# The norms ahead of two MLPs: from a stage of their own into the MLPs' first two chunks

## The chip, the cores and the metric

One core of one Trainium2 chip runs one program. The metric is the device time of that program in microseconds (us). A core has TensorE (PE in the profile, with its weight loads as PEld), VectorE (DVE), ScalarE (ACT), GpSimd (POOL), and SyncE (SP), which here only issues DMAs. Each engine works through its own list of instructions in order; they meet only in counters ("semaphores") that an instruction raises and another waits for.

## The reference, cut to what matters

Four layers are applied in turn to x, four batches of 512 tokens by 512 features. The second and the third layer each end in an MLP with a norm ahead of it, and these two places are changed:

```python
def ada_rms(x, t, w, tw):                       # layer 1
    n = x * jax.lax.rsqrt(jnp.mean(jnp.square(x), axis=-1, keepdims=True) + EPS)
    scale = t @ tw.T
    return n * (w * (1.0 + scale))[:, None, :]
h = ada_rms(x, time_emb, ln2_w, ln2_tw)
mlp = jax.nn.silu(h @ Wg.T) * (h @ Wu.T) @ Wd.T     # 512 -> 2048 -> 512
return res + mlp

def _ln(x):                                      # layer 2
    m = jnp.mean(x, axis=-1, keepdims=True)
    v = jnp.mean((x - m) ** 2, axis=-1, keepdims=True)
    return (x - m) / jnp.sqrt(v + LN_EPS)
h = _gelu_tanh((_ln(x) * (scale2 + 1.0) + shift2) @ Wfc1.T + bfc1)
x = x + (h @ Wfc2.T + bfc2) * gamma2
```

Everything is float32. Each batch needs only its own norm.

## The kernel before, in words

x lies in SBUF with the features on the partitions, as four tiles of 128 x 512 per batch (tile c is `k.xs(b, c)`). A sum over features is then a matmul with a matrix of 1/512 (`k.ones`), which also spreads the result over all partitions, into one bank of PSUM.

The program is a list of phases. A phase starts on an engine only when all engines have ended the phase before it, apart from a few instructions that a norm is let ahead by. The phases are: the conditioning vectors; `layers01` (all of layer 0 and the attention of layer 1, one woven sequence); `norm1b`, four norms, one per batch; `mlp1`; `layer2` (the attention of layer 2, woven); `norm2b`, four norms; `mlp2`; `layer3`. "Woven" means a Python list of (stage, batch, engine, operation) from which each engine takes its own operations in the list's order; waits are derived from what an operation reads.

A norm (class `Norm`) ahead of MLP 1 does, per batch: four squares on ACT into `k.t1` (L117), four matmuls with `k.ones` that sum them (L87, two fp32 passes each), the square root on ACT (L119), a reciprocal on DVE (L99), four scalings on DVE (L102), then for each tile a rounded copy "high" on ACT (L132) and the rest "low" on DVE (L109). High and low together carry float32 through the faster matmul type: the MLP multiplies high by high, high by low and low by high (`three`). The norm ahead of MLP 2 is a layer norm: it has four matmuls for the mean first (L81) and four subtractions (L96), a shift on ACT after the scaling (L124), and on ACT the addition of a bias to x itself (L136).

An MLP (class `Mlp`) cuts its 2048 hidden features into 8 chunks. A step is one chunk j for one batch q; the steps run j outermost: (0,0), (0,1), (0,2), (0,3), (1,0) and so on, 32 steps. A step's up matmuls fill tiles t = 0 and 1 of the hidden layer (L970; 48 matmuls of 128x512 with a gate, in MLP 1, 24 without, in MLP 2). ACT applies silu or gelu (L996, L998), DVE multiplies by the other half in MLP 1 (L1029), ACT makes high (L1004) and DVE low (L1035). The down matmuls (L983, 24 of them) run one step later, and DVE adds each of their four results to x (L1043). The chunk's weights arrive by a DMA of SP, and DVE splits them into high and low as well (L1016, L1021): chunk 0 before the first step, chunk j+1 during chunk j.

## Time and profile before

| | us |
|---|---|
| median of 3 runs | 2855.88 (2855.48 to 2857.81) |
| the profiled execution, its own time | 2853.02 |
| its span | 2851.0 |
| PE busy | 2561.1 (90%) |
| DVE busy | 1257.6 (44%) |
| ACT busy | 1133.4 (40%) |
| POOL busy | 263.4 (9%) |
| mean granted clock of TensorE | 0.943 of full |

The span runs from the first to the last instruction of the profile; 2.0 us of the execution lie around it. A time in the rows below counts from the span's start. "Busy" adds up the durations of an engine's instructions; TensorE's clock is given as a share of 2.4 GHz, and 0.50 is its lower level of 1.2 GHz.

### The profile page before, as it was taken

What the parts mean: (1) busy time and instruction counts of PE and PEld (TensorE: products, weight loads), DVE (VectorE), ACT (ScalarE), POOL (GpSimd) and SP (SyncE); (2) the same over time, 40 slices, a digit from 0 to 9 for tenths busy, and PEclk for the clock granted to TensorE, in tenths of its full rate; (3) what the DMA queues carried; (4) which work ended last, traced back from release to release, by engine and by line L of the source; (5) the groups of instructions that cost most, each with busy time, mean ns of one, the idle gap of its engine ahead of it and who ended that gap; (6) DMA issues with size and microseconds to landing.
All of it is one profiled execution on the core that took longest, in us unless ns stands there. A gap on an engine that the chain in (4) does not pass through costs nothing.

```text
span 2851.0 us, 32766 instructions
## 1 busy us (share of the span) xinstructions
PE 2561.1 (90%) x13072; PEld 1549.5 (54%) x13072; DVE 1257.6 (44%) x2490; ACT 1133.4 (40%) x2422; POOL 263.4 (9%) x233
## 2 busy tenths in 40 slices
...
DMA packets 35687, 61.24 MB, mean 21 GB/s; under 512 B 5184, under 2 KB 18032, under 8 KB 35024
## 3 DMA queue, kind: packets, MB, share of 16 engines
...
## 4 chain that ended last, share of the span: by engine, by line
PE 53%; DVE 5%; ACT 5%; issue 0%; POOL 0%; DVEq 0%; ACTq 0%; POOLq 0%
PE banks L970 18%; PE banks L983 12%; PE banks L441 10%; PE banks L682 3%; PE banks L675 2%; PE banks L695 2%; PE banks L527 1%; DVE sb_Pr L740 1%; DVE sb_PT L747 1%; PE banks L81 1%; PE banks L598 1%; ACT sb_Pr L765 1%; PE banks L591 1%; PE banks L87 1%; ACT sb_experts L609 1%; DVE sb_Pb L99 0%
## 5 line engine op out<-in xcount | busy, mean ns | idle before, releaser
L970 PE MATMUL banks<-sb_H,sb_Ws 128*128 128x512 f32 x2304 | 536.9, 391 | 31.1 <-DVE sb_Ws L1021 30.9
L970 PEld LDWEIGHTS banks<-sb_H,sb_Ws 128*128 128x128 f32 x2304 | 435.2, 189 | 123.8 <-issue 32.5
L765 ACT ACTIVATE sb_Pr<-sb_Pr,sb_nmax 128x512 f32<-128x512 f32 (+3 forms) x512 | 326.0, 638 | 117.4 <-DVE sb_nmax L740 115.2
L682 PEld LDWEIGHTS banks<-sb_ident,sb_Pr 128*128 128x128 f32 x2176 | 251.6, 147 | 210.4 <-issue 90.0
L682 PE MATMUL banks<-sb_ident,sb_Pr 128*128 128x128 f32 x2176 | 327.5, 292 | 28.2 <-ACT sb_PT L770 21.9
L675 PE MATMUL banks<-sb_R 32*128 32x512 f32 (+4 forms) x1280 | 305.9, 602 | 45.1 <-DVE sb_nmax L740 30.3
L747 DVE COPY sb_PT<-banks 128x512 f32<-128x512 f32 (+3 forms) x320 | 195.3, 610 | 333.4 <-PE banks L682 330.8
L740 DVE CUSTOM_DVE_ANT_0 sb_Pr<-banks,sb_bias 128x512 f32<-128x512 f32 (+3 forms) x512 | 290.9, 581 | 92.9 <-PE banks L675 91.9
L983 PE MATMUL banks<-sb_hidH,sb_Ws 128*128 128x512 f32 x1024 | 325.2, 389 | 0.0
L770 ACT ACTIVATE sb_PT<-banks 128x512 f32<-128x512 f32 (+3 forms) x320 | 169.2, 529 | 349.5 <-PE banks L682 348.8
L441 PE MATMUL banks<-sb_hN,sb_W 128*128 128x512 f32 x576 | 273.3, 622 | 12.3 <-ACT sb_hN L382 9.6
L675 PEld LDWEIGHTS banks<-sb_R 32*128 32x128 f32 (+1 forms) x1280 | 105.3, 192 | 200.4 <-issue 80.8
L983 PEld LDWEIGHTS banks<-sb_hidH,sb_Ws 128*128 128x128 f32 x1024 | 192.1, 188 | 39.8
L983 PE MATMUL banks<-sb_hidL,sb_Ws 128*128 128x512 f32 x512 | 199.2, 389 | 0.0
L441 PEld LDWEIGHTS banks<-sb_hN,sb_W 128*128 128x128 f32 x576 | 110.7, 201 | 138.1 <-issue 125.1
L1035 DVE TENSOR_TENSOR sb_hidL<-sb_hN,sb_hidH 128x512 fp32r<-128x512 f32 x128 | 88.6, 692 | 205.8 <-ACT sb_hidH L1004 205.8
L441 PE MATMUL banks<-sb_A,sb_W 128*128 128x512 f32 x384 | 174.6, 600 | 3.4 <-DVE sb_hN L482 3.4
L695 PE MATMUL banks<-sb_PT,sb_V 128*32 128x256 f32 (+2 forms) x2304 | 169.7, 381 | 1.8 <-DVE sb_rsum L751 0.9
L1004 ACT ACTIVATE sb_hidH<-sb_hN 128x512 fp32r<-128x512 f32 x128 | 80.9, 632 | 186.3 <-DVE sb_hN L1029 184.2
L1029 DVE TENSOR_TENSOR sb_hN<-sb_t,banks 128x512 f32<-128x512 f32 x64 | 44.0, 687 | 247.9 <-PE banks L970 195.5
L998 ACT ACTIVATE sb_hN<-banks,sb_cols 128x512 f32<-128x512 f32 x64 | 44.0, 688 | 248.4 <-PE banks L970 248.4
L996 ACT ACTIVATE sb_t<-banks 128x512 f32<-128x512 f32 x64 | 38.3, 599 | 245.7 <-PE banks L970 245.7
...
## 6 DMA issues: line engine op xcount, KB each, us to landing
sb_WM<-in_L_cond_Wfc SPq DMA_DIRECT2D x16, 512.0 KB, 4.2
...
sb_WM<-in_L_cond_Wg SPq DMA_DIRECT2D x8, 512.0 KB, 3.4
sb_WM<-in_L_cond_Wu SPq DMA_DIRECT2D x8, 512.0 KB, 4.4
sb_WM<-in_L_cond_Wd SPq DMA_DIRECT2D x8, 512.0 KB, 3.6
...
```

The source lines that it names most:

```text
L441: mm = e.matmul(bank[:, columns], lhsT, rhs, start=start, stop=stop)
L675: mm = e.matmul(k.bank(n % 4)[:, 0:s.width(u)], s.q(b, c)[rows, i * P:(i + 1) * P], s.k(b, c)[rows, 0:s.width(u)], start=True, stop=True)
L682: mm = e.transpose(bank[:, j * P:(j + 1) * P], k.Pr[:, n % 6, j * P:(j + 1) * P], k.ident[:])
L695: mm = e.matmul(bank[rows, 2 * P * ip + skip:2 * P * (ip + 1)], s.v(b, j, s.vhead(c, hl)), s.PT[:, n % 2, hl, j, skip:2 * P], start=j == 0 ...
L740: ins = e.tensor_tensor_reduce(k.Pr[:, n % 6, 0:s.width(u)], S, k.bias[:, s.units[u][2], 0:s.width(u)], -1.0, 3.0e38, ALU.add, ALU.min, s. ...
L747: ins = e.tensor_copy(*s.turned(k, b, u))
L765: ins = e.activation(prob, prob if s.biased else k.bank(n % 4)[:, 0:s.width(u)], ACT.Exp, bias=s.stat(k, k.nmax, b, u), scale=-1.0 if s.bi ...
L770: ins = e.activation(*s.turned(k, b, u), ACT.Copy)
L970: mm = e.matmul(k.bank(s.ups * t + w), lhsT, rhs, start=i == 0, stop=i == len(mats) - 1)
L983: mm = e.matmul(k.bank(4 + m), lhsT, rhs, start=i == 0, stop=i == len(mats) - 1)
L1004: ins = e.activation(k.hidH[:, st % 2, t, :], k.hN[:, 2 * (st % 2) + t, :], ACT.Copy)
L1035: ins = e.tensor_tensor(k.hidL[:, st % 2, t, :], k.hN[:, 2 * (st % 2) + t, :], k.hidH[:, st % 2, t, :].bitcast(F32), ALU.subtract)
```

## The change

The class `Norm` (and the unused `Linear` and `joined`) goes. `PairNorm` takes its place as a stage of a woven sequence, and each MLP becomes such a sequence that holds its norms.

- The order of the steps: chunks 0 and 1 go batch by batch, (0,0), (1,0), (0,1), (1,1), (0,2), (1,2), (0,3), (1,3), and from chunk 2 on j is outermost as before.
- The norm of batch 0 stands ahead of the first step, with the split of chunk 0 between its parts. The norm of batch q+1 is cut into parts ("beats") that follow, one each, the parts of steps (0,q) and (1,q); what is left when step (1,q) ends follows there.
- The split of chunk 1 stands at the end of step (0,0), and that of chunk 2 at the end of step (1,3).
- The sums over the four tiles are made on POOL (three additions of tiles), and one matmul with `k.ones` replaces four. In the first MLP POOL adds the squares; in the second it adds x and the squares.
- 1/sqrt(v) is exp(-0.5 ln v), both on ACT, in place of a square root on ACT and a reciprocal on DVE.
- The tiles of the norm: `nt`, two new ones, for sums, logarithm and inverse root; for the scaled values one new tile `nh` in MLP 1 (each c waits for the low of c-1), and `t1` in MLP 2. The norm's matmuls use bank 7 in MLP 1, which the down matmuls of m = 3 use too, and bank 2 in MLP 2.
- A matmul group "up" of step (j,q) waits for the high and the low of all four tiles of batch q.
- All else in the diff is a change of form (`after` returns what to wait for, and the caller waits).

```diff
-class Norm(Step):
...
+class PairNorm:
+    def beats(s, b):
+        tail = [[("pe", "var", 0), ("act", "log", 0), ("act", "inverse", 0)]]
+        for c in range(C):
+            last = [("dve", "scale", c)] + ([] if s.rms else [("act", "shift", c)])
+            last += [("act", "high", c), ("dve", "low", c)]
+            tail.append(last + ([("act", "extra", c)] if s.extra else []))
+        squares = [[("act", "square", c)] + ([("pool", "vsum", c)] if c else []) for c in range(C)]
+        if s.rms:
+            return squares + tail
+        return [[("pool", "xsum", i) for i in range(3)], [],
+                [("pe", "mean", 0)] + [("dve", "centre", c) for c in range(C)]] + squares + tail
...
+    def pe(s, k, e, b, kind, i, after):
+        bank = s.tab.claim(e, s, b, kind, i, after)
+        for due in after(s.name, b, *(("xsum", 2) if kind == "mean" else ("vsum", C - 1))):
+            e.wait_ge(*due)
+        e.matmul(bank, k.ones[:], k.nt[:, 0, :], start=True, stop=True).then_inc(k.done["pe"], 1)
...
+    def act(s, k, e, b, kind, c, after):
...
+            if c > 1:
+                for due in after(s.name, b, "vsum", c - 1):
+                    e.wait_ge(*due)
+            ins = e.activation(n1 if c else n0, s.x(b, c) if s.rms else s.h(c), ACT.Square)
...
+            ins = e.activation(n1, s.tab.at[(s.name, b, "var", 0)], ACT.Ln, bias=s.eps, scale=1.0)
...
+            ins = e.activation(n0, n1, ACT.Exp, scale=-0.5)
...
-        s.S = NCH * B
...
+        s.steps = [(j, q) for q in range(B) for j in range(2)] + [(j, q) for j in range(2, NCH) for q in range(B)]
+        s.at_step = {jq: st for st, jq in enumerate(s.steps)}
...
+    def sequence(s):
+        splits = {}
+        for j in range(2, NCH):
+            free, first = s.at_step[(j - 2, B - 1)] + 1, s.at_step[(j, 0)]
+            for p in range(len(s.pieces)):
+                splits.setdefault(min(free + 1 + p % 2, first - 1), []).extend(s.split(j)[2 * p:2 * p + 2])
+        splits[0] = s.split(1)
+        lead, first = s.norm.beats(0), s.split(0)
+        seq = []
+        for i in range(max(len(lead), len(first))):
+            seq += [(s.norm, 0, *op) for op in (lead[i] if i < len(lead) else [])]
+            seq += [(s, 0, *op) for op in first[i:i + 1]]
+        waiting = []
+        for st in range(len(s.steps) + 1):
+            parts = []
+            if st < len(s.steps):
+                j, q = s.steps[st]
+                for t in range(2):
+                    parts.append([("pe", "up", (st, t, w)) for w in range(s.ups)] + [("act", "act", (st, t))] +
+                                 ([("dve", "gate", (st, t))] if s.gated else []) +
+                                 [("act", "hidden high", (st, t)), ("dve", "hidden low", (st, t))])
+                if j == 0 and q + 1 < B:
+                    waiting = [[(s.norm, q + 1, *op) for op in ops] for ops in s.norm.beats(q + 1)]
+            if st >= 1:
+                parts += [[("pe", "down", (st - 1, m)), ("dve", "add", (st - 1, m))] for m in range(C)]
+            parts.append(splits.get(st, []))
+            for ops in parts:
+                seq += [(s, 0, *op) for op in ops]
+                if waiting:
+                    seq += waiting.pop(0)
+            if st < len(s.steps) and s.steps[st][0] == 1:
+                for ops in waiting:
+                    seq += ops
+                waiting = []
+        return seq
...
-        norm1b = [Norm(k.xs, combc(1), None, eps6[:, 0:1], rms=True, pair=(k.HH, k.HL))]
+        norm1b = PairNorm("norm1b", k.xs, lambda c: k.nh[:, 0, :], combc(1), None, eps6[:, 0:1], k.HH, k.HL, rms=True)
...
-        norm2b = [Norm(k.xs, modc(28), modc(36), eps6[:, 0:1], pair=(k.HH, k.HL), extra=combc(2))]
+        norm2b = PairNorm("norm2b", k.xs, lambda c: k.t1[:, c, :], modc(28), modc(36), eps6[:, 0:1], k.HH, k.HL,
+                          extra=combc(2))
...
+        mlp1, woven_mlp1 = mlp("mlp1", True, split1, [(0, 2 * C * HC), (2 * C * HC, 2 * D)], 1, norm1b, 7)
+        mlp2, woven_mlp2 = mlp("mlp2", False, split2, [(0, 2 * C * HC)], 2, norm2b, 2,
+                               hbias=col["L2_cond_bfc1"], gamma=modc(20))
```

Three places show how the instructions now stand. The first is DVE in the second step of MLP 1. Before, that step, (0,1), held gate (L1029), low (L1035), the split of chunk 1's first piece (L1016, L1021) and the four additions to x (L1043):

```order
L1029 TENSOR_TENSOR sb_hN<-sb_t,banks 128x512
L1035 TENSOR_TENSOR sb_hidL<-sb_hN,sb_hidH 128x512
L1029 TENSOR_TENSOR sb_hN<-sb_t,banks 128x512
L1035 TENSOR_TENSOR sb_hidL<-sb_hN,sb_hidH 128x512
L1016 CAST sb_Ws<-sb_WM 128x2048
L1021 TENSOR_TENSOR sb_Ws<-sb_WM,sb_Ws 128x2048
L1043 SCALAR_TENSOR_TENSOR sb_x<-banks,sb_x 128x512 x4
```

Now the second step, (1,0), holds the end of batch 1's norm; a piece of its start stands here, from the split of chunk 1 (L1056, L1060) on. L1070 is the gate, L1079 the hidden low, L1092 an addition to x, L922 the scaling of one tile of the norm and L927 its low:

```order
L1056 CAST sb_Ws<-sb_WM 128x1024
L1060 TENSOR_TENSOR sb_Ws<-sb_WM,sb_Ws 128x1024
L1070 TENSOR_TENSOR sb_hN<-sb_t,banks 128x512
L1079 TENSOR_TENSOR sb_hidL<-sb_hN,sb_hidH 128x512
L1070 TENSOR_TENSOR sb_hN<-sb_t,banks 128x512
L1079 TENSOR_TENSOR sb_hidL<-sb_hN,sb_hidH 128x512
L1092 SCALAR_TENSOR_TENSOR sb_x<-banks,sb_x 128x512
L922 SCALAR_TENSOR_TENSOR sb_nh<-sb_x,sb_comb,sb_nt 128x512
L927 TENSOR_TENSOR sb_H<-sb_nh,sb_H 128x512
L1092 SCALAR_TENSOR_TENSOR sb_x<-banks,sb_x 128x512
L922 SCALAR_TENSOR_TENSOR sb_nh<-sb_x,sb_comb,sb_nt 128x512
```

Each addition is now followed by a scaling and a low of the norm, four times in a row, before DVE comes to the next step's gate.

The second place is DVE in MLP 2, with batch 2's norm in step (1,1). Before, in the same place of the list, there are only hidden lows (L1035), additions (L1043) and a split:

```order
L1035 TENSOR_TENSOR sb_hidL<-sb_hN,sb_hidH 128x512 x2
L1043 SCALAR_TENSOR_TENSOR sb_x<-banks,sb_mod,sb_x 128x512 x4
L1035 TENSOR_TENSOR sb_hidL<-sb_hN,sb_hidH 128x512 x2
L1016 CAST sb_Ws<-sb_WM 128x2048
L1021 TENSOR_TENSOR sb_Ws<-sb_WM,sb_Ws 128x2048
L1043 SCALAR_TENSOR_TENSOR sb_x<-banks,sb_mod,sb_x 128x512 x4
```

Now the four subtractions of the mean (L912) stand among step (0,1)'s additions, and the scalings and lows among those of step (1,1):

```order
L1092 SCALAR_TENSOR_TENSOR sb_x<-banks,sb_mod,sb_x 128x512
L912 TENSOR_TENSOR sb_t<-sb_x,banks 128x512 x4
L1092 SCALAR_TENSOR_TENSOR sb_x<-banks,sb_mod,sb_x 128x512 x3
L1079 TENSOR_TENSOR sb_hidL<-sb_hN,sb_hidH 128x512 x2
L922 SCALAR_TENSOR_TENSOR sb_t<-sb_t,sb_mod,sb_nt 128x512
L927 TENSOR_TENSOR sb_H<-sb_t,sb_H 128x512
L1092 SCALAR_TENSOR_TENSOR sb_x<-banks,sb_mod,sb_x 128x512
L922 SCALAR_TENSOR_TENSOR sb_t<-sb_t,sb_mod,sb_nt 128x512
L927 TENSOR_TENSOR sb_H<-sb_t,sb_H 128x512
```

The pattern of the last three rows goes on until all four tiles are done.

The third place is ACT in the same steps. Before, the norms stood together ahead of the MLP, where ACT went from one table of functions to the next once (L119 is the root, L124 the shift, L132 high, L136 the addition to x, L998 gelu, L1004 hidden high):

```order
L119 ACTIVATE sb_Pb<-banks,sb_eps 128x512
L124 ACTIVATE sb_hN<-sb_hN,sb_mod 128x512 x4
L132 ACTIVATE sb_H<-sb_hN 128x512 x4
L136 ACTIVATE sb_x<-sb_x,sb_comb 128x512 x4
L998 ACT_TABLE_LOAD
L998 ACTIVATE sb_hN<-banks,sb_cols 128x512
L1004 ACTIVATE sb_hidH<-sb_hN 128x512
```

Now the logarithm (L886) and the exponential (L890) stand between two gelus (L1034), with a table load ahead of each of the three; L882 is a square, L894 the shift, L898 high, L902 the addition to x, L1042 hidden high:

```order
L1034 ACTIVATE sb_hN<-banks,sb_cols 128x512
L1042 ACTIVATE sb_hidH<-sb_hN 128x512
L886 ACT_TABLE_LOAD
L886 ACTIVATE sb_nt<-banks,sb_eps 128x512
L890 ACT_TABLE_LOAD
L890 ACTIVATE sb_nt<-sb_nt 128x512
L1034 ACT_TABLE_LOAD
L1034 ACTIVATE sb_hN<-banks,sb_cols 128x512
L1042 ACTIVATE sb_hidH<-sb_hN 128x512
L894 ACTIVATE sb_t<-sb_t,sb_mod 128x512
L898 ACTIVATE sb_H<-sb_t 128x512
L902 ACTIVATE sb_x<-sb_x,sb_comb 128x512
```

The second gelu of the step now comes behind the exponential and a table load.

## Rows read from the trace of the kernel before

**Rows 1.** Busy time by stretch: before and in each MLP; stretch and length, engines (instructions), PEclk.

```profile
1002.60:1065.50 62.90, 21.53 (x33) 8.38 (x33) 40.03 (x41) 22.86 (x37) 0.00 (x0) 0.70 0.09 29
1065.50:1589.80 524.30, 524.21 (x2304) 433.59 (x2304) 205.87 (x284) 80.10 (x129) 0.00 (x0) 1.00 0.07 21
2268.70:2350.80 82.10, 36.58 (x65) 13.99 (x63) 48.53 (x55) 42.34 (x69) 0.00 (x0) 0.76 0.18 51
2350.80:2702.10 351.30, 351.06 (x1536) 289.90 (x1536) 158.45 (x205) 85.76 (x129) 0.00 (x0) 0.99 0.05 19
```

**Rows 2.** Timeline, norms ahead of MLP 1: start, length, engine, line, what [idle <-releaser].

```profile
1002.65 0.69 DVE L1314 SCALAR_TENSOR_TENSOR sb_x<-banks,sb_x 128x512 f32<-128x512 f32 x1 [2.74 <-PE banks L441]
...
1003.90 0.51 SPq L1606 DMA_DIRECT2D sb_WM<-in_L_cond_Wu  x1
...
1059.96 1.23 DVE L1016 CAST sb_Ws<-sb_WM 128x2048 fp32r<-128x2048 f32 x1
...
1064.15 1.23 DVE L1021 TENSOR_TENSOR sb_Ws<-sb_WM,sb_Ws 128x1024 fp32r<-128x1024 f32 x1
...
1065.52 23.73 PE L970 MATMUL banks<-sb_H,sb_Ws 128*128 128x512 f32 x96 [15.04 <-DVE sb_Ws L1021]
```

**Rows 3.** Groups of instructions: DVE in 1003:1066, then ACT in 2268:2351 (mean ns).

```profile
L102 DVE SCALAR_TENSOR_TENSOR sb_hN<-sb_x,sb_comb,sb_Pb 128x512 f32<-128x512 f32 x16 | 11.0, 748 | 0.1
...
L124 ACT ACTIVATE sb_hN<-sb_hN,sb_mod 128x512 f32<-128x512 f32 x16 | 10.8, 722 | 16.8 <-DVE sb_hN L102 16.8
```

**Rows 4.** Timeline, first norm of the kernel: POOL sums, TensorE, logarithm and exponential.

```profile
93.11 1.26 POOL L358 TENSOR_TENSOR sb_t<-sb_t 128x512 f32<-128x512 f32 x1
...
102.62 2.08 PE L342 MATMUL banks<-sb_t,sb_ones 128*128 128x512 f32 x2 [6.05 <-POOL sb_t L358]
104.73 0.69 ACT L376 ACTIVATE sb_Pb<-banks,sb_eps 128x512 f32<-128x512 f32 x1 [3.58 <-PE banks L342]
105.43 1.28 ACT L379 ACT_TABLE_LOAD   x1
106.73 0.63 ACT L379 ACTIVATE sb_Pb<-sb_Pb 128x512 f32<-128x512 f32 x1
```

**Rows 5.** DMA issues, us to landing: in 1000:1030, then in 2265:2300.

```profile
sb_WM<-in_L_cond_Wu SPq DMA_DIRECT2D x1, 512.0 KB, 5.2
...
sb_WM<-in_L_cond_Wfc SPq DMA_DIRECT2D x4, 512.0 KB, 5.3
```

**Rows 6.** Timeline of two steps in MLP 1, then of one in MLP 2.

```profile
1078.48 0.69 DVE L1029 TENSOR_TENSOR sb_hN<-sb_t,banks 128x512 f32<-128x512 f32 x1 [3.36 <-PE banks L970]
1079.20 0.63 ACT L1004 ACTIVATE sb_hidH<-sb_hN 128x512 fp32r<-128x512 f32 x1 [2.91 <-DVE sb_hN L1029]
1079.87 0.69 DVE L1035 TENSOR_TENSOR sb_hidL<-sb_hN,sb_hidH 128x512 fp32r<-128x512 f32 x1 [0.70 <-ACT sb_hidH L1004]
...
1094.82 0.68 DVE L1043 SCALAR_TENSOR_TENSOR sb_x<-banks,sb_x 128x512 f32<-128x512 f32 x1
...
2359.11 5.69 PE L970 MATMUL banks<-sb_H,sb_Ws 128*128 128x512 f32 x24 [0.17 <-ACT sb_hidH L1004]
...
2362.12 0.69 ACT L998 ACTIVATE sb_hN<-banks,sb_cols 128x512 f32<-128x512 f32 x1 [1.79 <-PE banks L970]
```

**Rows 7.** Timeline, around the norms ahead of MLP 2.

```profile
2268.76 0.75 DVE L1314 SCALAR_TENSOR_TENSOR sb_x<-banks,sb_mod,sb_x 128x512 f32<-128x512 f32 x1 [2.68 <-PE banks L441]
...
2270.06 0.50 SPq L1618 DMA_DIRECT2D sb_WM<-in_L_cond_Wfc  x1
...
2285.23 6.62 PE L81 MATMUL banks<-sb_x,sb_ones 128*128 128x512 f32 x8 [7.69 <-ACT sb_hN L124]
```

**Rows 8.** Granted clock by stretch, where the MLPs begin.

```profile
1066.00:1072.00 6.00, 6.00 (x21) 4.74 (x20) 0.00 (x0) 1.68 (x2) 0.00 (x0) 0.74 0.56 196
...
2350.00:2356.00 6.00, 5.16 (x12) 4.12 (x13) 0.70 (x1) 0.00 (x0) 0.00 (x0) 0.50 0.50 175
```

**Rows 9.** Timeline of TensorE in layer 3.

```profile
2741.78 5.33 PE L441 MATMUL banks<-sb_Y,sb_Wout 128*128 128x512 f32 x8 [3.14 <-ACT sb_Y L382]
```

732 lines of the change are left out of this document (358 added, 374 removed).

## The prediction, as it was put on record

> **What bounds the kernel now.** I read three views. The busy time by stretch comes first [rows 1]: in both MLPs TensorE is busy all the time (524.21 of 524.30 us, 351.06 of 351.30), and ahead of each lies a stretch in which it mostly waits for a norm, 62.9 and 82.1 us. That is the 145.0 us the change works on; all else in the 2853.0 us stays as it is. The timeline comes second [rows 2, 7]: the last addition to x of the layer before ends at 1003.3 (2269.5), MLP 1's first matmul starts at 1065.52, MLP 2's at 2350.8. The third, single rows of one pass of each kind, gives durations [rows 3, 4, 6]. MLP 1's 2304 matmuls in 524.3 us are 0.227 us each: 24 of them (one tile's ups with a gate, or a step's downs) take 5.44.
>
> So TensorE sets the end inside an MLP, and the question is what it waits for when norms stand there too. I take ends and starts from the rows: TensorE to another engine 0.29 (2359.11 + 12 x 0.227 to 2362.12 [rows 6]), another engine to TensorE 0.14 (1065.38 to 1065.52 [rows 2]), ACT to DVE or back 0.03 [rows 6], into or out of POOL 0.10. Passes of 128x512: scale 0.75, shift 0.72 [rows 3], high 0.63, low 0.69 [rows 6], POOL addition 1.26 [rows 4], a square as the exponential, 0.63. The 0.10 for POOL is an allowance of mine.
>
> **The lead, batch 0's norm.** MLP 1: two squares, three POOL additions, two more squares between them: 1003.4 + 1.25 + 3 x 1.37 + 2 x 0.66 = 1010.1. The one matmul took 2.08 on a TensorE that had paused [rows 4], to 1012.3; logarithm 0.69, table load 1.28, exponential 0.63 follow each other without a gap there (104.73, 105.43, 106.73), to 1015.0. The weights' split takes 5.42 (1059.96 to 1065.38) and starts when the DMA issued at 1003.90 has landed, 5.2 later [rows 5]: 1014.6, just hidden. Then four tiles in a chain, since one `nh` serves all and DVE queues low c ahead of scale c+1: 0.75+0.63+0.69+3x0.03 = 2.16 each, 8.6. Ups start at 1023.7 instead of 1065.5: **-41.8**.
>
> MLP 2: DVE's list has the split (3.56) ahead of the subtractions; its DMA, issued at 2270.06, lands after 5.3, so they start at 2278.9. The first square starts 0.8 later; two squares take 1.25, three POOL additions with two squares between them 5.4, the matmul 2.2, logarithm to exponential 2.65: 2291.2. The additions for the mean, 3 x 1.26 from 2269.6, and its matmul end earlier than the split. A tile's chain has the shift too: 2.91 each, 11.6. Ups at 2302.95 instead of 2350.8: **-47.9**.
>
> **What comes back, step by step.** Let U be the time when a step's ups end on TensorE. Its last hidden low ends at U + 2.35 (0.29 + 0.69 + 0.63 + 0.69 and two 0.03).
>
> - Step (0,0) to (1,0). Chunk 1's split is queued on DVE behind that low, and step (0,0) has no downs to cover it. MLP 1: 2.35 + 5.42 + 0.14 = **+7.9**. MLP 2: 2.35 + 3.56 + 0.14 = **+6.05**.
> - MLP 1, batch 1's norm, in step (1,0). The matmul stands right behind the ups, ACT does high (to U+1.6), loads a table, and has the exponential done at U+5.55. Then DVE alternates additions and tiles: 4 x 2.16 + 3 x 0.71 = 10.8, with 0.14 to U+16.45. The downs need 5.44: **+11.0**.
> - MLP 1, batches 2 and 3: their parts start a step earlier. TensorE, in order, comes to the norm's matmul at U+4.1, and POOL's last sum is ready at U+7.75 (high ends at 1.65, then three squares of 0.66 and three additions of 1.37). The matmul is 0.9, and the next down shares bank 7, so it waits for the logarithm, 0.95. The tiles themselves are hidden behind a whole step. 5.5 each: **+11.0**.
> - Chunk 2's split stands at the end of step (1,3), behind the last addition: 0.96 + 5.42 + 0.14 = **+6.55**; MLP 2 0.29 + 0.75 + 3.56 + 0.14: **+4.7**.
> - MLP 2, batch 1's norm: a layer norm has 12 parts, and step (0,0) takes only three, so all squares stand in step (1,0). The sum is ready at U+7.75 as above, the matmul takes 1.0, logarithm to exponential 2.65, and then come four tiles (11.6), nearly all behind the step's last addition: next ups at U+23.15, own work 5.44: **+17.7**.
> - MLP 2, batches 2 and 3. The squares follow the subtractions behind step (0,q)'s first addition, the sum is ready at U+10.6, exponential at U+14.7; the second gelu of step (1,q) is queued behind it with a table load, its low ends at U+18.1. Only then does the first tile start: 4 x 2.91 + 3 x 0.78 + 0.14 to U+32.2. TensorE has 3 x 5.44 to do in between: **+15.85** each, 31.7.
>
> Sum: MLP 1 -41.8 + 7.9 + 11.0 + 11.0 + 6.55 = -5.3. MLP 2 -47.9 + 6.05 + 17.7 + 31.7 + 4.7 = +12.3. Together **+7**. The POOL additions, the reciprocals that go (eight) and the 36 matmuls that go are counted in the leads or hidden; POOL has nothing else to do there (0.00 busy [rows 1]), and the DMAs of later chunks are issued as early as before or earlier.
>
> **The clock.** TensorE's granted clock is at its lower level, 1.2 GHz, after the waits ahead of an MLP (0.50 of full [rows 8]). The first 24 ups of MLP 2 took 8.10 where the next 24 took 5.69 [rows 6, 7], and MLP 1's first 96 took 23.73 for 21.8 [rows 2]: 2 to 2.7 lost per return. After 7.69 us of idling eight matmuls ran 6.62 us for about 3.5 at the full clock [rows 7], after 3.14 us in a loose stretch eight took 5.33 [rows 9]. Five of the new pauses are 7.9 us or longer (MLP 1's first two, one per batch in MLP 2): 2.3 each, 11.5. Three last about 4.7 to 6.5: no row says which way they go, from 0 to 2.7 each, and I take half, 3.5. Clock: **+15**, bounds 0 and 27 (ten pauses of 2.7, with those of 3.7 us ahead of a sum).
> The page "TensorE: Matmul & The Clock Gate" of the Trainium skill, section "HAM oscillation", tells of a loop whose every round starts at the lower clock because each round has a pause. By that rule every pause here would be paid, the upper bound; the trace agrees for the long ones.
>
> **The table loads.** In the trace a load costs its 1.28 and nothing more: the logarithm ends at 105.42, the exponential starts at 106.73 [rows 4]. About eight of the new loads stand on the path (the exponential's in both leads, in both batches 1 and in MLP 2's batches 2 and 3, and there gelu's too).
> The Trainium skill, "ScalarE: Activation LUTs", section "What ACT_TABLE_LOAD costs", adds a drain of about 1.38 us to each switch, 2.66 in all. By it the sum would be 11 higher. The trace disagrees.
>
> **Forecast.** 2853.0 + 7 + 15 = 2875 for the profiled execution; the median of the runs lies 2.9 above it, so **2878**. Slower.
>
> **Rivals.**
> 1. *The norms are hidden* (the faster side). If the tiles' chain of batches 1 to 3 ended before the downs did, all that is left of the price is the splits and the nine matmuls: 2856 - 90 + 25 + 9 = 2800. For it: ACT is busy 80 of 524 us in MLP 1 and DVE 206 [rows 1], so there is room on average. Against: the list gives DVE the tiles only among or behind the last downs. It decides in MLP 2, at batches 2 and 3: were the first tile there 15.9 us earlier, the sum without the clock would turn from +7 to -25. 4%.
> 2. *The clock holds through the new pauses.* 2856 + 7 = 2863. For it: only average rows speak of how TensorE behaves between 3 and 7 us. Against: 7.69 us cost it. 12%.
> 3. *Every pause costs the clock*, and waits on POOL are longer than I took: 7 + 27 = 2890. 14%.
> 4. *The chains overlap more than I count*, DVE's next scaling under ACT's work, 2 us less per norm and half the clock: 2856 - 7 + 7 = 2856, no change. 8%. *Some piece outruns its chain by more*, faster by over 0.2%: 3%, beside rival 1.
>
> Forecast itself 59%. Two runs of this kernel differ by under 0.1%; 0.2% is 5.7 us, what a measurement can tell from none. Faster 0.07 (rival 1 and the last), same 0.10 (rival 4 and the edge of 2), slower 0.83. The range goes from below rival 2 to rival 3: 2857 to 2891.
>
> **What would show it.** TensorE's first up at about 20 us after the layer before in MLP 1 and 33 in MLP 2; between the first steps pauses of 8 and 11 us in MLP 1, 6, then 13, 12, 12 in MLP 2, ended by DVE's low of a norm (L927) or a split (L1060); MLP 1 from the last addition before it to its end about as long as before, MLP 2 some 20 us longer; a clock at half in the first stretch behind each pause. It is wrong if TensorE's waits for L927 sum to under 30 us, or if the ups start later than 1030 and 2310.

## The result, and the profile after

The changed kernel takes 2884.15 us (median of 4 runs, 2882.56 to 2887.32) against 2855.68 us (4 runs, 2853.25 to 2857.81): ratio 1.0102, 95% interval 1.0087 to 1.0117. It is slower by 28.5 us; 22 were forecast. The profiled execution took 2882.56 us (span 2880.6).

Busy time by stretch of the changed kernel, one core; columns are stretch and length, then busy time (and instructions) of PE, PEld, DVE, ACT, POOL, then PEclk, DMA share, GB/s. The four stretches are MLP 1's lead and the rest of MLP 1, then the same of MLP 2. They answer to [rows 1].

```profile
1005.49:1026.74 21.25, 2.05 (x3) 0.53 (x3) 12.06 (x12) 9.68 (x13) 4.66 (x3) 0.61 0.45 148
1026.74:1600.30 573.56, 540.01 (x2310) 441.53 (x2310) 227.08 (x307) 109.07 (x168) 11.65 (x9) 0.96 0.05 17
2275.43:2309.72 34.29, 3.69 (x4) 0.83 (x5) 12.39 (x15) 15.37 (x21) 10.63 (x9) 0.57 0.52 153
2309.72:2732.90 423.18, 370.71 (x1548) 300.36 (x1548) 184.17 (x241) 131.05 (x192) 20.69 (x16) 0.93 0.04 13
```

The reader is to see three things. The leads are short now: 21.25 us where 62.2 lay between the same two events (1003.3 to 1065.5), 34.3 where there were 81.3. Behind them TensorE, which never waited inside an MLP before, is idle for 573.56 - 540.01 = 33.6 us in MLP 1 and 423.18 - 370.71 = 52.5 in MLP 2. And it is busy longer for the same work: 540.0 us, less 3 for the norms' three matmuls (two passes each, six of the 2310), against 524.2, and 370.7, less 6.2 for six matmuls, against 351.1. That is 12.8 and 13.4 us, 26.2 together, and its granted clock says why: 0.96 and 0.93 instead of 1.00 and 0.99.

From the last addition of the layer before to its last matmul, MLP 1 takes 594.8 us (586.4 before), MLP 2 457.5 (432.6). So the two stages lose 33.3; the layers that the change does not touch came out 3.7 shorter in this execution (layer 2 took 675.1 us instead of 679.8).

Where TensorE waits, in the timeline of the changed kernel; columns are start, length, engine, line, operation, out<-in, count, [idle before <-releaser]. L844 is a norm's matmul, L1016 an MLP's, L927 DVE's low of a norm, L1060 the split, L866 a POOL addition.

```profile
1026.74 13.01 PE L1016 MATMUL banks<-sb_H,sb_Ws 128*128 128x512 f32 x48 [11.52 <-DVE sb_H L927]
1049.42 13.54 PE L1016 MATMUL banks<-sb_H,sb_Ws 128*128 128x512 f32 x48 [9.67 <-DVE sb_Ws L1060]
...
1078.64 12.64 PE L1016 MATMUL banks<-sb_H,sb_Ws 128*128 128x512 f32 x48 [9.35 <-DVE sb_H L927]
1098.69 1.88 PE L844 MATMUL banks<-sb_nt,sb_ones 128*128 128x512 f32 x2 [3.34 <-POOL sb_nt L866]
...
2323.22 7.83 PE L1016 MATMUL banks<-sb_H,sb_Ws 128*128 128x512 f32 x24 [4.86 <-DVE sb_Ws L1060]
2338.61 2.05 PE L844 MATMUL banks<-sb_nt,sb_ones 128*128 128x512 f32 x2 [3.48 <-POOL sb_nt L866]
2356.35 8.30 PE L1016 MATMUL banks<-sb_H,sb_Ws 128*128 128x512 f32 x24 [13.14 <-DVE sb_H L927]
...
2396.77 8.53 PE L1016 MATMUL banks<-sb_H,sb_Ws 128*128 128x512 f32 x24 [12.53 <-DVE sb_H L927]
...
2436.45 7.54 PE L1016 MATMUL banks<-sb_H,sb_Ws 128*128 128x512 f32 x24 [11.55 <-DVE sb_H L927]
2449.27 5.60 PE L1016 MATMUL banks<-sb_H,sb_Ws 128*128 128x512 f32 x24
2464.71 7.07 PE L1016 MATMUL banks<-sb_H,sb_Ws 128*128 128x512 f32 x24 [4.40 <-DVE sb_Ws L1060]
```

Ahead of the first steps stand the pauses that the prediction names, ended by the lines it names. Behind each, 24 ups take 7 to 8.5 us and 48 take 12.6 to 13.5; where nothing paused 24 take 5.60, as at 2449.27, and 48 took 11.04 (at 1121.21).

### The profile page after: what moved, and what is told of

It reads as the page before. It is cut to its first block, busy times and chain, and to the rows that moved or that the text cites. A ratio compares the mean times of both kernels' runs of the same rounds, so it can differ in the third digit from the quotient of the medians.

```text
span 2880.6 us, 32059 instructions
## 1 busy us (share of the span) xinstructions
PE 2538.5 (88%) x13000; PEld 1542.2 (54%) x13000; DVE 1242.2 (43%) x2482; ACT 1169.2 (41%) x2450; POOL 311.1 (11%) x269
## 4 chain that ended last, share of the span: by engine, by line
PE 76%; DVE 9%; ACT 9%; POOL 2%; DMA 2%; issue 1%; SPq 0%; DVEq 0%; POOLq 0%; ACTq 0%
PE banks L1016 30%; PE banks L299 20%; PE banks L568 8%; PE banks L560 6%; PE banks L584 5%; DVE sb_PT L641 2%; PE banks L594 2%; DVE sb_Pr L634 2%; PE banks L335 1%; ACT sb_Pr L663 1%; PE banks L395 1%; PE banks L1259 1%; ACT sb_PT L668 1%; DMA sb_WM<-in_L_cond_W_ada 1%; PE banks L474 1%
## 5 line engine op out<-in xcount | busy, mean ns | idle before, releaser
L1016 PE MATMUL banks<-sb_H,sb_Ws 128*128 128x512 f32 x2304 | 556.6, 401 | 98.4 <-DVE sb_H L927 73.2
L1016 PEld LDWEIGHTS banks<-sb_H,sb_Ws 128*128 128x128 f32 x2304 | 448.0, 195 | 201.4 <-issue 71.5
L1016 PE MATMUL banks<-sb_hidH,sb_Ws 128*128 128x512 f32 x1024 | 331.3, 394 | 1.6 <-ACT sb_nt L886 1.6
L1016 PEld LDWEIGHTS banks<-sb_hidH,sb_Ws 128*128 128x128 f32 x1024 | 193.9, 189 | 46.3 <-ACT sb_nt L886 4.7
L1016 PE MATMUL banks<-sb_hidL,sb_Ws 128*128 128x512 f32 x512 | 200.6, 392 | 0.0
L1079 DVE TENSOR_TENSOR sb_hidL<-sb_hN,sb_hidH 128x512 fp32r<-128x512 f32 x128 | 88.7, 693 | 224.2 <-ACT sb_hidH L1042 224.2
L1042 ACT ACTIVATE sb_hidH<-sb_hN 128x512 fp32r<-128x512 f32 x128 | 81.1, 634 | 183.4 <-DVE sb_hN L1070 181.4
L1070 DVE TENSOR_TENSOR sb_hN<-sb_t,banks 128x512 f32<-128x512 f32 x64 | 44.0, 688 | 235.3 <-PE banks L1016 235.3
L1034 ACT ACTIVATE sb_hN<-banks,sb_cols 128x512 f32<-128x512 f32 x64 | 44.1, 689 | 249.4 <-PE banks L1016 249.4
```

Source lines behind the costliest of these rows:

```text
L1016: mm = e.matmul(bank, lhsT, rhs, start=i == 0, stop=i == len(mats) - 1)
L1042: ins = e.activation(k.hidH[:, st % 2, t, :], k.hN[:, 2 * (st % 2) + t, :], ACT.Copy)
L1079: ins = e.tensor_tensor(k.hidL[:, st % 2, t, :], k.hN[:, 2 * (st % 2) + t, :], k.hidH[:, st % 2, t, :].bitcast(F32), ALU.subtract)
```

## The experiments

All start from the changed kernel (L numbers are those of each kernel). Medians, with the ratio to the kernel before:

| kernel | us | ratio, 95% interval | stage MLP 1 | stage MLP 2 |
|---|---|---|---|---|
| before | 2855.7 | 1 | 586.4 | 432.6 |
| changed | 2884.2 | 1.0102 (1.0087 to 1.0117) | 594.8 | 457.5 |
| a: chunk 1's split ahead | 2863.0 | 1.0032 (1.0017 to 1.0047) | 583.8 | 448.1 |
| c: tiles overlapped | 2856.2 | 0.9999 (0.9990 to 1.0009) | 588.3 | 436.4 |
| a and c | 2836.6 | 0.9932 (0.9914 to 0.9949) | 577.0 | 428.6 |
| d: waits filled | 2877.7 | 1.0078 (1.0061 to 1.0095) | 589.9 | 453.3 |
| b: norms in front | 2887.7 | 1.0112 (1.0097 to 1.0127) | 591.6 | 464.1 |
| b and c | 2854.5 | 1.0008 (0.9996 to 1.0020) | 582.6 | 444.4 |
| g: sums on TensorE | 2877.2 | 1.0080 (1.0063 to 1.0097) | 586.9 | 454.2 |
| i: chunk 2's split early | 2873.4 | 1.0063 (1.0047 to 1.0079) | 586.5 | 448.5 |
| r: root by reciprocal | 2896.6 | 1.0130 (1.0102 to 1.0158) | 600.9 | 454.3 |
| e: norms earlier | 2767.9 | 0.9705 (0.9684 to 0.9725) | 544.6 | 391.9 |
| e, leads filled | 2766.1 | 0.9686 (0.9671 to 0.9701) | 544.3 | 391.2 |

The stages are from the profiled execution, from the end of the last addition of the layer before to the end of the last matmul of the MLP. A difference behind "Measured" is that of two medians, most of them of four executions. The kernel before, run 18 times beside a, b, c and d, gave 2852.3 to 2858.9 us, so a few us of such a difference can be chance; the intervals of the changed kernel and of d, b, g and r overlap. Layer 2 has the same code in all, and it alone took from 673.1 to 685.7 us in the profiled executions.

### Chunk 1's split ahead

```diff
-        splits[0] = s.split(1)
...
+        seq += [(s, 0, *op) for op in s.split(1)]
         waiting = []
         for st in range(len(s.steps) + 1):
```

> Chunk 1's split is queued ahead of the first step instead of behind it, in both MLPs; nothing else changes. Theory (each wait of TensorE costs its own length and then some 2 us of lower clock): in MLP 1 the pause of 9.86 us ahead of step (1,0) goes, and with it 2.4 us of slow ups behind it; in MLP 2 the 5.9 us pause and about 2. Sum -20, 2864 us (2860 to 2869). Rival (the waits are one chain: a wait that goes comes back at batch 1's norm, whose tiles are as late as before): MLP 1's gain shrinks to under 4 us and the wait ahead of step (0,1) grows from 15.9 toward 22; the time stays above 2875.

Measured 2863.0, -21.1. The waits ahead of step (1,0) are gone in both MLPs, and the wait ahead of (0,1) did not grow: 9.34 us after 9.35 in MLP 1, 13.15 after 13.14 in MLP 2. In MLP 1, 96 ups follow one another; this row of the kernel's timeline is the one to compare with the first two above, which took 13.01 + 9.67 + 13.54:

```profile
1028.92 23.78 PE L1016 MATMUL banks<-sb_H,sb_Ws 128*128 128x512 f32 x96 [11.51 <-DVE sb_H L927]
```

So the split was a term of its own, worth 21 us; 14.5 of them are the two waits (9.67 and 4.86), and TensorE was busy 4.7 us less in the two MLPs (538.8 and 367.2 us after 540.0 and 370.7), which is the clock.

### The tiles of a norm overlapped

```diff
-        for c in range(C):
-            last = [("dve", "scale", c)] + ([] if s.rms else [("act", "shift", c)])
-            last += [("act", "high", c), ("dve", "low", c)]
-            tail.append(last + ([("act", "extra", c)] if s.extra else []))
+        ahead = 2 if s.rms else C
+        for c in range(C):
+            last = [("dve", "scale", i) for i in range(C) if (i < ahead if c == 0 else i == c + ahead - 1)]
+            last += [] if s.rms else [("act", "shift", c)]
+            tail.append(last + [("act", "high", c), ("dve", "low", c)])
+        if s.extra:
+            tail[-1] += [("act", "extra", c) for c in range(C)]
...
-            elif c or b:
-                for due in after(s.name, b if c else b - 1, "low", (c - 1) % C):
+            elif c > 1 or b:
+                for due in after(s.name, b if c > 1 else b - 1, "low", (c - 2) % C):
...
-norm1b = PairNorm("norm1b", k.xs, lambda c: k.nh[:, 0, :], ...
+norm1b = PairNorm("norm1b", k.xs, lambda c: k.t1[:, 2 + c % 2, :], ...
```

> The four tiles of a norm overlap: in MLP 2 all four scalings are queued on DVE ahead of the first low, and the additions of the bias to x (L902) behind the last tile; in MLP 1 a tile has two buffers and DVE queues scale 0, scale 1, low 0, scale 2, low 1 and so on. Theory (DVE's in-order alternation of scale and low is what makes a tile cost 2.9 us in MLP 2 and 2.16 in MLP 1): MLP 2's lead and its three waits ahead of (0,1) to (0,3) shrink by 4.5 us each, MLP 1's lead by 2.9, batch 1's wait there by 2: -23, 2861 us (2856 to 2867). Rival (the exponential and its table load, or the additions of the downs, end last anyway): the three waits in MLP 2 shrink by under 2 us each, and the time stays above 2874.

Measured 2856.2, -27.9: equal to the kernel before. DVE between the exponential and the next ups of batch 2 in MLP 2, first the scalings of two tiles in the changed kernel, then all four tiles in this one:

```profile
2382.36 0.75 DVE L922 SCALAR_TENSOR_TENSOR sb_t<-sb_t,sb_mod,sb_nt 128x512 f32<-128x512 f32 x1
...
2385.83 0.74 DVE L922 SCALAR_TENSOR_TENSOR sb_t<-sb_t,sb_mod,sb_nt 128x512 f32<-128x512 f32 x1
```

```profile
2366.26 2.73 DVE L925 SCALAR_TENSOR_TENSOR sb_t<-sb_t,sb_mod,sb_nt 128x512 f32<-128x512 f32 x4
2368.91 0.68 DVE L930 TENSOR_TENSOR sb_H<-sb_t,sb_H 128x512 fp32r<-128x512 f32 x1
...
2370.17 1.10 DVE L930 TENSOR_TENSOR sb_H<-sb_t,sb_H 128x512 fp32r<-128x512 f32 x1
...
2371.86 1.09 DVE L930 TENSOR_TENSOR sb_H<-sb_t,sb_H 128x512 fp32r<-128x512 f32 x1
...
2373.53 1.09 DVE L930 TENSOR_TENSOR sb_H<-sb_t,sb_H 128x512 fp32r<-128x512 f32 x1
```

Four scalings in a row, then a low every 1.3 to 1.7 us (an addition to x stands between two lows), where one tile followed the other after 3.47 us: a tile costs less than half of what it did. The waits in MLP 2 fell from 13.14, 12.53, 11.55 to 9.24, 6.61, 5.35; in MLP 1 the lead's last wait from 11.52 to 8.55 and batch 1's from 9.35 to 6.32. The stages fell by 21.1 us in MLP 2 and 6.5 in MLP 1, where the expectation has 18 and 5; the three waits fell by 3.9, 5.9 and 6.2 instead of 4.5 each.

### Both

> a_split_ahead and c_tiles_overlap together, nothing else. Theory (the two waits are separate terms of one sum): the gains add, 2884 - 21 - 28 = 2835 us (2830 to 2841), and the rest of the way to e_stream (2768), 67 us, is the earlier start of batches 1 to 3 and chunk 2's split. Rival (a wait that goes makes another longer): 2842 or more.

Measured 2836.6. The gains add (2884.2 - 21.1 - 27.9 = 2835.2): these two groups of waits are separate terms of one sum, as the prediction took them.

### Waits filled with idle matmuls

```diff
+            if not s.gated and j == 0 and q and t == 0:
+                for _ in range(44):
+                    e.matmul(bank, k.HH(0, 0)[:, 0:P], k.HH(0, 1), start=True, stop=True)
...
+        if s.rms and b >= 2:
+            for _ in range(14):
+                e.matmul(bank, k.HH(0, 0)[:, 0:P], k.HH(0, 1), start=True, stop=True)
```

> TensorE's waits are filled with matmuls whose result is overwritten, and nothing else changes: 44 (10 us) behind the wait's start ahead of the first ups of (0,1), (0,2) and (0,3) in MLP 2 (waits of 13.1, 12.5, 11.6 us), 14 (3.2 us) ahead of the sum's matmul of batches 2 and 3 in MLP 1 (waits of 3.4 us). Theory (the lower clock behind a wait is the wait's own price): the 24 ups behind the three waits take 5.5 to 6 us instead of 8.30, 8.53 and 7.54, and in MLP 1 the sum's matmul 1.0 to 1.2 instead of 1.9 and the 6 us behind it run at full clock: -7 in MLP 2, -4 in MLP 1, 2873 us (2869 to 2877). Rival (the clock falls for another reason, a budget over the whole MLP, or the fill runs past the wait and delays the real work): the ups behind stay at 7.5 or longer, 2884 us or more.

Measured 2877.7, -6.5. In MLP 1 the wait of 3.34 us is filled with 3.33 us of matmuls. First the changed kernel there (busy by stretch, 6 us from the first down behind the norm's matmul, batches 2 and 3, and 6 us behind chunk 2's split), then the same place with the filling:

```profile
1101.00:1107.00 6.00, 5.65 (x16) 4.47 (x17) 1.98 (x3) 2.85 (x4) 0.00 (x0) 0.60 0.00 1
1142.00:1148.00 6.00, 5.53 (x16) 4.39 (x17) 1.86 (x3) 2.97 (x4) 0.00 (x0) 0.61 0.00 0
1201.00:1207.00 6.00, 5.73 (x18) 4.62 (x19) 0.12 (x1) 0.60 (x1) 0.00 (x0) 0.69 0.68 237
1207.00:1213.00 6.00, 6.00 (x29) 4.95 (x28) 1.38 (x2) 1.23 (x2) 0.00 (x0) 1.00 0.00 0
```

```profile
1098.30:1104.30 6.00, 5.96 (x26) 4.94 (x27) 2.83 (x5) 3.23 (x5) 0.00 (x0) 1.00 0.00 1
1136.60:1142.60 6.00, 6.00 (x26) 4.97 (x27) 2.88 (x5) 3.24 (x5) 0.00 (x0) 1.00 0.01 3
```

16 matmuls in 6 us at 0.60 of the clock against 26 at 1.00. The lower of the two levels, 1.2 GHz, is thus the wait's own doing, and a wait of 3.3 us was enough. Where the clock falls differs a little: in the changed kernel the sum's matmul right behind the wait takes 1.88 us already (1.13 with the filling), in kernel a it takes 1.12 behind a wait of 3.33, and the clock falls only behind it, where TensorE waits another 0.78; the downs that follow run at 0.50 in both. In MLP 2 the 44 matmuls took 10.1 us and left part of the wait. The kernel's timeline there:

```profile
2339.72 10.13 PE L1004 MATMUL banks<-sb_H 128*128 128x512 f32 x44
2353.10 7.14 PE L1022 MATMUL banks<-sb_H,sb_Ws 128*128 128x512 f32 x24 [3.24 <-DVE sb_H L930]
...
2379.68 10.13 PE L1004 MATMUL banks<-sb_H 128*128 128x512 f32 x44
2392.36 7.32 PE L1022 MATMUL banks<-sb_H,sb_Ws 128*128 128x512 f32 x24 [2.54 <-DVE sb_H L930]
```

After the rests of 3.24 and 2.54 us the ups still took 7.14 and 7.32; after the third, of 1.56 us, 5.72. So MLP 2 gained 4.2 us instead of 7, and the expectation was wrong there (2877.7 is just outside its range too): the filling shortened the waits and did not end them, and the clock was low behind the two longer rests all the same. The price of one wait also varies from kernel to kernel: behind the whole, unfilled waits the same three groups of 24 took 7.17, 7.97 and 7.21 us in kernel a, so only the 5.72 is clearly the filling's.

### The norm's form apart from its place

```diff
-        s.steps = [(j, q) for q in range(B) for j in range(2)] + [(j, q) for j in range(2, NCH) for q in range(B)]
+        s.steps = [(j, q) for j in range(NCH) for q in range(B)]
...
+        for q in range(1, B):
+            seq += [(s.norm, q, *op) for ops in s.norm.beats(q) for op in ops]
         waiting = []
```

> The changed norm in the old place: all four batches' norms ahead of step 0, one after the other, and the chunks outermost, so that only the order of the work is as in the kernel before, not the way a norm is summed and its root taken. Theory (a norm in the new form is a serial chain of some 18 us in MLP 1 and 23 in MLP 2, longer than one in the kernel before, where it was 15 and 20): leads of 21 + 3 x 18 = 75 us (62 before) and 34 + 3 x 20 = 94 (81 before), then no pause but chunk splits, -0 to 10 us on each MLP: 2856 + 13 + 13 = 2882 us (2870 to 2895). So most of the loss would be the norm's form, and the new place gives back what it costs. Rival (the form is as good as the old one, and the loss comes from the new place): leads of 62 and 81, 2856 us (2850 to 2865).

Measured 2887.7. In the old place the new norm costs 32 us more than the old one. The new place as such makes 3.5 us (2887.7 to 2884.2), and the two intervals overlap: moving the norms, with chunk 1's and chunk 2's splits where the change puts them, gave back in waits and clock what it took from the leads. So the form alone is as large as the loss. By the stages it is mostly MLP 2's: the form adds 5.2 us in MLP 1 and 31.5 in MLP 2 (10 of them are a wait ahead of the second step's ups), and the new place then adds 3.2 in MLP 1 and takes 6.6 in MLP 2. TensorE's timeline ahead of MLP 1 has one norm every 19.2 us, since the next norm's squares wait for the last scaling of this one (they share `nt`); over the four the kernel before needed 62.2 (15.5 each):

```profile
1012.99 2.05 PE L844 MATMUL banks<-sb_nt,sb_ones 128*128 128x512 f32 x2 [8.36 <-POOL sb_nt L866]
1032.19 2.05 PE L844 MATMUL banks<-sb_nt,sb_ones 128*128 128x512 f32 x2 [17.16 <-POOL sb_nt L866]
1051.40 2.05 PE L844 MATMUL banks<-sb_nt,sb_ones 128*128 128x512 f32 x2 [17.16 <-POOL sb_nt L866]
1070.60 2.05 PE L844 MATMUL banks<-sb_nt,sb_ones 128*128 128x512 f32 x2 [17.16 <-POOL sb_nt L866]
```

The expected 75 and 94 us of leads came out as 66 (1005.4 to 1071.7, whose first ups overlap the last norm) and 101.6; in MLP 2 a norm's period is 27.9.

> The two edits before together: all norms ahead of the first step (as in b_norms_front) and the four tiles of a norm overlapped (as in c_tiles_overlap). Theory (what makes the new norm dearer than the old in the same place, 2888 against 2857, is the chain of its four tiles through one buffer and DVE's order): a norm's period falls from 19.2 to 16.3 us in MLP 1 and from 27.9 to 23.5 in MLP 2, the time to 2888 - 12 - 17 = 2859 (2853 to 2865), about the kernel before. Rival (the POOL sums and the two table loads make it dearer): the periods fall by under 1.5 us each, the time stays above 2877.

Edit: both diffs above. Measured 2854.5, -33.2: as fast as the kernel before. The periods fell to 16.25 and 22.35 us. So the chain of the four tiles accounts for about the whole difference in this place, and what POOL's additions and the table loads cost beside the four matmuls and the reciprocal is small against it. How small stays open: the median says 1 us less than before, the two stages of the profiled execution say 8 more (3.8 less in MLP 1, 11.8 more in MLP 2). With the tiles overlapped the place makes about as little as without: 2854.5 in the old one, 2856.2 in the new one.

### The parts of the form

Sums on TensorE:

```diff
-        e.matmul(bank, k.ones[:], k.nt[:, 0, :], start=True, stop=True).then_inc(k.done["pe"], 1)
+        for c in range(C):
+            if kind == "var":
+                for due in after(s.name, b, "square", c):
+                    e.wait_ge(*due)
+            mm = e.matmul(bank, k.ones[:], s.x(b, c) if kind == "mean" else s.square(k, c), start=c == 0, stop=c == C - 1)
+        mm.then_inc(k.done["pe"], 1)
```

> The changed kernel with its sums taken by four matmuls each on TensorE (squares in four buffers), as in the kernel before, instead of POOL additions and one matmul. Theory (POOL's serial additions of 1.26 us each make the sum late, and slow DVE beside them): the waits of 3.4 us ahead of the sum in MLP 1's batches 2 and 3 and batch 1 of MLP 2 go, the split in MLP 1's step (0,0) takes 5.4 instead of 7.4, the squares are done 3.5 us earlier; against it 3 more matmuls of 0.46 to 0.9 us per sum, 12 sums. Sum -12, 2872 us (2864 to 2878). Rival (the sum is not what ends last, the matmuls cost what POOL saved): 2882 to 2890.

Measured 2877.2, -7.0: inside the range given, but half of the sum (the two stages give 11.2, while layer 2 took 4.5 more). The waits ahead of the sums of batches 2 and 3 in MLP 1 are gone; the four matmuls take about 3.6 us (1093.57 to 1097.17 for batch 2) where one took 1.0 to 1.9, and in MLP 2 batches 2 and 3 gain nothing: 41.6 and 42.9 us from ups to ups, 40.4 and 39.7 with POOL.

POOL idle beside the split (the norm's parts start in step (1,0) of MLP 1: `if waiting and (st or not s.gated)`):

> In MLP 1's step (0,0) nothing of batch 1's norm stands any more (it starts in step (1,0)), so POOL is idle while DVE splits chunk 1. Theory (DVE's two-input passes and casts run slower while POOL adds): the CAST of 2.30 us takes 1.23, the subtraction of 3.23 takes 2.29, and the pause ahead of step (1,0) is 7.9 us instead of 9.86. Batch 1's norm then ends later, so the whole may be 2 to 6 us slower; the pause is what is read. Rival (they are slow because of the weights' DMA that lands at the same time): still 2.3 and 3.2, and 9.9.

One execution, 2888.1 us. DVE's timeline in step (0,0), first the changed kernel with POOL beside it, then this one:

```profile
1041.80 1.26 POOL L866 TENSOR_TENSOR sb_nt<-sb_nt 128x512 f32<-128x512 f32 x1 [28.77 <-ACT sb_nt L882]
1041.84 2.30 DVE L1056 CAST sb_Ws<-sb_WM 128x2048 fp32r<-128x2048 f32 x1
...
1043.80 1.46 POOL L866 TENSOR_TENSOR sb_nt<-sb_nt 128x512 f32<-128x512 f32 x1 [0.74 <-ACT sb_nt L882]
1044.18 3.23 DVE L1060 TENSOR_TENSOR sb_Ws<-sb_WM,sb_Ws 128x2048 fp32r<-128x2048 f32 x1
```

```profile
1044.54 1.22 DVE L1056 CAST sb_Ws<-sb_WM 128x2048 fp32r<-128x2048 f32 x1
1045.80 2.29 DVE L1060 TENSOR_TENSOR sb_Ws<-sb_WM,sb_Ws 128x2048 fp32r<-128x2048 f32 x1
```

TensorE's wait is 7.65 instead of 9.67 us. The longer times are those of waiting for POOL and then running as alone: POOL's addition ends at 1041.80 + 1.26 = 1043.06, and 1.22 later, at 1044.28, the cast would be done (it is at 1044.14); 1043.80 + 1.46 + 2.29 = 1047.55 for the subtraction (1047.41). With the sums on TensorE these two passes take 1.22 and 2.29 as well. The Trainium skill, "SBUF — State Buffer", section "SBUF: two separate sides", has this rule: DVE and GpSimd share a pair of ports, taken as a lock for a whole instruction, by DVE in a two-port mode or, against a GpSimd operation that reads SBUF, with two SBUF inputs. The trace agrees, to 0.14 us.

The root:

```diff
-            ins = e.activation(n1, s.tab.at[(s.name, b, "var", 0)], ACT.Ln, bias=s.eps, scale=1.0)
+            ins = e.activation(n1, s.tab.at[(s.name, b, "var", 0)], ACT.Sqrt, bias=s.eps, scale=1.0)
...
+        elif kind == "inverse":
+            for due in after(s.name, b, "log", 0):
+                e.wait_ge(*due)
+            ins = e.reciprocal(k.nt[:, 0, :], k.nt[:, 1, :])
```

> The changed kernel with the root taken as in the kernel before: square root on ACT, reciprocal on DVE, in place of logarithm and exponential. Theory (the price is 1.28 us of table load and 0.63 of exponential on ACT against 3.35 us of reciprocal on DVE, and both stand in the chain): each of the norms whose tiles end last (both leads, batch 1 in MLP 1, batches 1 to 3 in MLP 2: six) is 1.4 us later, +8 to +9, 2893 us (2889 to 2897); in batches 2 and 3 of MLP 1 the downs still wait for the root's reader on ACT alone. Rival (the table loads with a drain of their own cost more than the reciprocal): not slower, 2884 or less.

Measured 2896.6, +12.4 (runs from 2884.2 to 2899.5, a wide spread). The stages give +6.1 and -3.2; layer 2, whose code is the same, took 10.6 us more in the profiled execution. Both leads and both batches 1 wait longer, by 2.4 and 1.4 and by 1.8 and 1.3; MLP 2's batches 2 and 3 wait 1.4 shorter, because ACT has one table load less ahead of the gelu that their tiles are queued behind. So the median lies in the range expected, but not for the reason given: in the stages there are 3 us where the expectation has 8 to 9. That the reciprocal makes the chain of a lead or of batch 1 longer is shown; that logarithm and exponential are better for the whole kernel is not.

### Chunk 2's split beside the ups

```diff
-        for j in range(2, NCH):
+        for j in range(3, NCH):
...
+            if st < len(s.steps) and s.steps[st] == (1, B - 1):
+                parts = parts[2:6] + [s.split(2)] + parts[:2]
```

> The changed kernel with one change of order: in step (1,3) the downs of (0,3) stand ahead of the ups, and chunk 2's split right behind them, so that it runs beside the ups. Theory (the pauses of 6.20 and 4.40 us ahead of step (2,0) are the split's, and each costs 1.5 to 2 us of lower clock behind it): both go, -14, 2870 us (2866 to 2874). Rival (the split only moves: its staged weights or the hidden tiles of step (1,3) come later and TensorE waits there): less than 6 us gained.

Measured 2873.4, -10.8. Both waits (6.20 and 4.40) are gone and no other took their place; the stages fell by 8.3 and 9.0, while the layers that the change does not touch took more in the profiled execution.

### The norms earlier

```diff
+                put(q + 1, n["mean"] + n["squares"][0] + n["squares"][1])
...
+                side = {"t0": n["squares"][2] + n["squares"][3], "end" if q == 0 else "m0": n["root"]}
+                if q:
+                    side.update({"m3": n["tiles"][0], "end": n["tiles"][1]})
...
+            if (j, q) == (1, B - 1):
+                parts = downs + [("split", s.split(2))] + ups
```

The first line stands ahead of the ups of step (0,q), "t0" is behind its first tile's ups, "m0" behind its first down, and the last two tiles follow the first ups of step (1,q). Batch q+1's sums of x are put behind step (0,q-1), in `sd` and `rstd`.

> A version put together from what the runs so far showed: chunk 1's split ahead, chunk 2's split beside the ups of step (1,3) (its downs come first), tiles overlapped, batch q+1's centring and first squares ahead of step (0,q) with the mean of x summed earlier in buffers of its own, and the root behind the first downs of step (0,q). Theory (the waits are the chain of each norm, which an earlier start hides): only the leads (18 and 25 us), some 6 us of batch 1's norm in MLP 1 and in MLP 2 and a few short ones are left: 2856 - 21 (split ahead) - 15 (chunk 2 and its clock) - 25 (waits of batches 1 to 3 and their clock) = 2795 us (2782 to 2815). Rival (ACT with its three table loads per norm or POOL becomes the bound in MLP 2, and the waits turn up at the hidden tiles): 2815 to 2840.

Measured 2767.9, ratio 0.9705: 87 us below the kernel before in the same runs, 116 below the changed one, and 27 better than forecast, below the range given. TensorE's groups in MLP 1 (busy and mean ns of one, then the idle time before them):

```profile
L1041 PE MATMUL banks<-sb_H,sb_Ws 128*128 128x512 f32 x1536 | 356.2, 391 | 9.2 <-DVE sb_H L925 9.2
L1041 PE MATMUL banks<-sb_hidH,sb_Ws 128*128 128x512 f32 x512 | 163.7, 391 | 0.0
L1041 PE MATMUL banks<-sb_hidL,sb_Ws 128*128 128x512 f32 x256 | 99.6, 389 | 0.0
L843 PE MATMUL banks<-sb_nt,sb_ones 128*128 128x512 f32 x8 | 5.1, 725 | 6.3 <-POOL sb_nt L860 6.3
```

All idle time left in MLP 1 is the lead's (6.3 + 9.2). In MLP 2 there remain, behind the lead, waits of 2.10, 2.29, 0.76 and 1.93 us. The forecast had left 6 us of waiting and its clock for batch 1 in each MLP, and 25 us for what batches 1 to 3 give back, where kernel c still waits 42 us for their norms. This is rival 1 of the prediction, the norms hidden, and it comes true once the tiles do not stand behind the downs. Of the 69 us from a and c together to this version, chunk 2's split alone gave 11 in its own run; the rest is that of several edits which no run takes apart.

> e_stream with matmuls whose result is overwritten in the last part of each lead (7 ahead of MLP 1's first ups; 3 ahead of the mean of batch 1 and 2 ahead of the first ups in MLP 2). Theory (the ups behind a lead are slow because TensorE had paused): the first 48 ups of MLP 1 take 11.2 instead of 13.5 us and the first 24 of MLP 2 5.8 instead of 7.8, 2764 us (2761 to 2767). Rival (the fill runs longer than the wait at the lower clock, or does not raise it): the ups start later or stay slow, 2768 or more.

Edit: as in the waits filled, with `k.ones` and a tile of x as operands. Measured 2766.1; the intervals of the two ratios overlap, so no difference. The 48 ups of MLP 1 took 11.46 instead of 13.52 us, but the lead became 1.8 us longer (18.6 after 16.9), as the filling ran past the wait. In MLP 2 the filling ended 2.23 us before the wait did, and the 24 ups took 7.32 us, where 5.8 was expected and 7.83 stood before. So neither filling gave its gain: one ended too late and one too early.

## Why the prediction was right, and where its sizes were off

- *The leads.* -41.8 and -47.9 forecast; -40.9 and -47.0 measured (62.2 to 21.25, 81.3 to 34.29). The waits ahead of the ups, 11.52 and 15.14 us, are ended by the low of the norm, as worked out.
- *Step (0,0) to (1,0).* 7.9 forecast, 9.67 measured in MLP 1. The price of the split was that of a DVE alone; POOL's additions beside it cost 2.0, which p_split_alone showed by taking them away. The prediction had no step for two engines at one port. In MLP 2 6.05 forecast and some 5.9 measured.
- *Batch 1.* +11.0 and +17.7 forecast. In MLP 1 9.35 us of waiting and 1.0 for the matmul: 10.35. In MLP 2 3.48 + 1.0 + 13.14 = 17.6.
- *Batches 2 and 3.* 5.5 each in MLP 1: 3.34 + 0.78 + 1.0 = 5.1. 15.85 each in MLP 2: 1.26 + 2 x 1.0 + 12.53 = 15.8, and 14.9 for the last. The place of the first tile, behind the second gelu with its table load (2380.36 in the trace, the scale at 2382.36), is where it was said to be.
- *Chunk 2.* 6.55 and 4.7: 6.20 and 4.40. Experiment i took both away.
- *The sum without the clock.* +7 forecast. MLP 1 -40.9 + 9.7 + 10.35 + 10.3 + 6.2 = -4.35, MLP 2 -47.0 + 5.9 + 17.6 + 30.7 + 4.4 = +11.6: +7.25.
- *The clock.* This term was mis-sized: 15 forecast, 26 measured (busy time above). The step that failed is "I take half" for the three waits of 4.7 to 6.5 us and nothing for those of 3.4. The trace has eleven waits of 3.3 us or more behind the leads, and 26 / 11 = 2.4 us each (kernels a, c and i give 2.3 to 2.4 in the same way), about the price that the prediction had for the long ones, from the 5.69 of [rows 6] and this row of the kernel before, which it quoted as 8.10:

```profile
2350.84 8.10 PE L970 MATMUL banks<-sb_H,sb_Ws 128*128 128x512 f32 x24 [15.90 <-DVE sb_Ws L1021]
```

  The upper bound named in the prediction, 27, was nearly reached. The section "HAM oscillation" of the page "TensorE: Matmul & The Clock Gate" of the Trainium skill, which would have every pause paid, was borne out by all these waits, and was the better forecast. The filled waits show the cause: the same downs at 1.00.
- *The rest.* 7.25 + 26 = 33.3, and the profiled execution was 29.5 slower: the other layers took 3.7 less, which no step of the change explains. So it is partly luck that the time came out only 6 us above the forecast, with a term that was 11 too small.
- *The table loads.* Taken at 1.28 without a drain, against what "ScalarE: Activation LUTs" of the Trainium skill, section "What ACT_TABLE_LOAD costs", says of a switch. With 1.38 more for each, the waits of MLP 2 would have been longer than measured by that much; they are shorter than forecast. The trace of the changed kernel has load, logarithm, load, exponential, load, gelu at 2375.11, 2376.41, 2377.12, 2378.41, 2379.06 and 2380.36, without a gap.
- *Rivals.* Rival 2 (the clock holds) is out: the clock did not hold, and the filled waits show why. Rival 3 was right in its clock and wrong in its POOL waits. Rival 4 is what c makes true by an edit.

What the prediction did not say is where the loss comes from. It priced the tiles at 2.16 and 2.91 us each as given; b, c and b with c show that this serial chain alone is as large as the whole loss of a change that takes 88 us from the leads. It is not the only such term: chunk 1's split in front of step (0,0) gives back 21 us too, and chunk 2's 11.
